# A first mixture's norm spread over other steps of a token-mixing loop, and real matmuls in the place of matmuls of zeros behind it

## The reference, cut to what matters

```python
h = h + _L0_attn_ref(_layernorm(h, axis=-1), ...)
h = h + _L0_ffn_ref(_layernorm(h, axis=-1), ...)

def _layernorm(x, axis=-1, eps=1e-05):
    m = jnp.mean(x, axis=axis, keepdims=True)
    v = jnp.var(x, axis=axis, keepdims=True)
    return (x - m) / jnp.sqrt(v + eps)

def _L0_ffn_ref(x, Wr, br, ln_g, ln_b, W1, b1, W2, b2):
    logits = xt @ Wr + br
    probs = jax.nn.softmax(logits, axis=-1)
    top_p, top_idx = jax.lax.top_k(probs, TOP_K)          # TOP_K = 2 of 8 experts
    mu = xt.mean(axis=-1, keepdims=True)
    var = ((xt - mu) ** 2).mean(axis=-1, keepdims=True)
    xn = (xt - mu) * jax.lax.rsqrt(var + LN_EPS)
    h = jax.nn.gelu(jnp.einsum('end,edh->enh', xe, W1) + b1[:, None, :], approximate=False)
    ...

def _pinv(a, iters=6):
    ...
    for _ in range(iters):
        az = a @ z
        z = 0.25 * z @ (13.0 * I - az @ (15.0 * I - az @ (7.0 * I - az)))
```

## Time and profile before

| what | value |
|---|---|
| median of three executions | 708.01 us |
| lowest and highest | 704.61, 708.11 us |
| the profiled execution's own time | 709.06 us |
| its span in the trace | 707.3 us |
| mean granted TensorE clock over the span | 0.972 of full |

### The profile page before, as it was taken

One profiled execution on the slowest core, in us unless ns is written; L12 is line 12 of the kernel. 1 busy time (PEld: TensorE's weight loads), 2 busy tenths in 40 slices (PEclk: granted clock), 3 DMA queues, 4 the chain that ended last, 5 costly groups with the idle time before them and its releaser, 6 DMA issues. The chain is left out here.

```text
span 707.3 us, 15186 instructions
## 1 busy us (share of the span) xinstructions
PE 662.3 (94%) x6053; PEld 509.3 (72%) x6053; DVE 408.3 (58%) x832; ACT 375.1 (53%) x1033; POOL 229.6 (32%) x204
## 2 busy tenths in 40 slices
PE   9988989999999999999989999789999999999895
PEld 5777888898989898989755555467666666658555
DVE  3457575758585757665742333346777777754331
ACT  4667685746565555565255555235554555546431
POOL 4074443535363534444300451032232222200001
PEclk9999999999999999999999999859999999997999
DMA  8200000000000000000000000000000000000000
GB/s 278 102 3 2 1 1 2 3 1 2 1 2 2 1 2 2 1 2 2 1 1 1 1 1 1 0 1 2 1 1 1 1 0 2 1 0 1 1 16 17
DMA packets 5214, 8.23 MB, mean 12 GB/s; under 512 B 3608, under 2 KB 4120, under 8 KB 4760
## 3 DMA queue, kind: packets, MB, share of 16 engines
q1 hardware_dynamic: 4552, 7.20, 3.1%
q10 hardware_dynamic: 592, 0.07, 0.1%
HBM read 6.71 MB, written 0.55 MB: 10 GB/s over the span
## 5 line engine op out<-in xcount | busy, mean ns | idle before, releaser
L1333 POOL TENSOR_TENSOR STD<-STD,NN 91x492 f32<-91x492 f32 (+1 forms) x96 | 104.1, 1101 | 148.3 <-DVE NN L1489 79.1
L940 PE MATMUL PS<-ST 128*91 128x123 f32 x768 | 92.4, 271 | 5.3 <-DVE ST L1495 5.3
L1489 DVE SCALAR_TENSOR_TENSOR NN<-ST,PS 91x492 f32<-91x492 f32 x96 | 62.9, 661 | 57.1 <-PE PS L940 56.8
L940 PEld LDWEIGHTS PS<-ST 128*91 128x91 f32 x768 | 83.5, 159 | 10.9 <-DVE ST L1495 6.9
L940 PE MATMUL PS<-NN 128*91 128x123 f32 (+1 forms) x768 | 88.4, 266 | 2.0 <-DVE NN L1489 2.0
L940 PEld LDWEIGHTS PS<-NN 128*91 128x91 f32 x768 | 81.0, 159 | 9.0 <-DVE NN L1489 5.4
L1980 PE MATMUL PS<-QR,KA 128*128 128x270 f32 x256 | 72.5, 414 | 0.0
L2096 DVE TENSOR_SCALAR CL<-PS,K 128x270 f32<-128x270 f32 x144 | 65.6, 495 | 9.9 <-PE PS L1980 4.5
L1495 DVE SCALAR_TENSOR_TENSOR ST<-PS,STD 91x492 f32<-91x492 f32 (+1 forms) x96 | 56.0, 599 | 26.3 <-POOL STD L1333 16.4
L1212 ACT ACTIVATE STD<-ST 91x492 f32<-91x492 f32 (+1 forms) x96 | 51.6, 569 | 36.0 <-DVE ST L1495 36.0
L2037 ACT ACTIVATE EX<-CL,NG 128x540 f32<-128x540 f32 x64 | 46.7, 741 | 32.8 <-DVE CL L2096 32.7
(11 more groups left out here) (347 smaller groups left out, 1215.7 us busy)
## 6 DMA issues: line engine op xcount, KB each, us to landing
TP<-taps SPq DMA_DIRECT2D x1, 1204.0 KB, 15.6
MA<-mat SPq DMA_DIRECT2D x1, 1120.0 KB, 7.6
MF<-mat SPq DMA_DIRECT2D x1, 1024.0 KB, 12.6
WI<-wide SPq DMA_DIRECT2D x1, 902.0 KB, 9.1
CO<-const SPq DMA_DIRECT2D x1, 512.0 KB, 16.0
MQ<-mat SPq DMA_DIRECT2D x1, 512.0 KB, 16.6
out<-OS SPq DMA_DIRECT2D x8, 45.0 KB
XA<-xpatch SPq DMA_DIRECT2D x1, 256.0 KB, 2.8
```

What stands on the lines that cost most here:

```text
L940: last = nc.tensor.matmul(PS[0:NL, PINV + q, h % 4 * SW + c0:(h % 4 + 1) * SW], x[:, h, 0:NL], x[:, h, c0:SW], start=True, stop=True)
L1333: nc.gpsimd.tensor_tensor(TD[:, 4 * q:4 * q + 4, c0:SW], SA[:, 4 * q:4 * q + 4, c0:SW], NN[0:NL, 4 * q:4 * q + 4, c0:SW], ALU.subtract).th ...
L1489: v.scalar_tensor_tensor(out=NN[0:NL, own, :], in0=ST[0:NL, b % 2, own, :], scalar=N_S, in1=heads4(PS[0:NL, PINV + q, 0:4 * SW]), op0=ALU. ...
```

## The change: pieces in other steps, and the scales' matmuls in the tail

Nothing is computed otherwise. The pieces of the norm stand behind other steps:

| piece | engine | step before | step after |
|---|---|---|---|
| `spreads` (variances) | TensorE | 5 | 6 |
| `rooted` | ScalarE | 6 | 8 |
| `router` | TensorE | 7 | 9 |
| `inverted` | VectorE | 7 | 9 |
| `widths` | ScalarE | 9 | 10 |
| `scales` | TensorE | 10 | in the tail, one pair at a time |
| `rescaled` | VectorE | 11, ahead of the second part of the rank | pair 0 behind that part, pairs 1 and 2 at the block's end |

The three calls of `spin` in the tail (12 matmuls of 512 columns) are gone. In their places stand `scale(0)`, `scale(1)` and `scale(2)`, with three matmuls of 90 columns each. The variances and roots of the fourth pair use bank `NORMS` in place of bank 1.

```diff
-                def scales():
-                    for p in EARLY:
-                        pe.wait_ge(sem("d_widened"), p + 1)
-                        spread(p, p).then_inc(sem("d_spread"), 1)
-
-                NORM = {1: centred, 5: spreads, 7: router, 10: scales}
+                def scale(p):
+                    pe.wait_ge(sem("d_widened"), p + 1)
+                    spread(p, p).then_inc(sem("d_spread"), 1)
+
+                NORM = {1: centred, 6: spreads, 9: router}
...
                 attend(B - 1, 0)
                 attend(B - 1, 1)
-                pe.wait_ge(sem("d_step"), 1)
-                spin(2, NORMS)
+                scale(0)
                 out_proj(B - 1)
-                spin(4, NORMS)
+                scale(1)
                 pe.wait_ge(sem("f_res"), upto(B - 1, 3, 3))
-                pe.wait_ge(sem("d_done"), BP - 1)
+                pe.wait_ge(sem("d_done"), 1)
                 centre(BP - 1, 0).then_inc(sem("d_centred"), 1)
                 pe.wait_ge(sem("d_squared"), BP)
-                variances(BP - 1, 1, KT * (BP - 1)).then_inc(sem("d_var"), 1)
-                spin(6, NORMS)
+                pe.wait_ge(sem("d_step"), 1)
+                variances(BP - 1, NORMS, KT * (BP - 1)).then_inc(sem("d_var"), 1)
+                scale(2)
...
-                NORM.update({2: squared, 6: lambda: rooted(EARLY, NORMS), 9: widths})
+                NORM.update({2: squared, 8: lambda: rooted(EARLY, NORMS), 10: widths})
...
-                NORM = {2: (kept_early,), 7: (inverted,), 10: (ranked_first,),
-                        11: (rescaled, lambda: ranked(dve, "d", EARLY, NORMS, 1))}
+                NORM = {2: (kept_early,), 9: (inverted,), 10: (ranked_first,),
+                        11: (lambda: ranked(dve, "d", EARLY, NORMS, 1), lambda: rescaled(0))}
...
                 residual(B - 1)
                 kept(BP - 1, 0)
+                rescaled(1)
+                rescaled(2)
```

More of the change, by code:

```diff
@@ L1312, in _ @@
                 squares(BP - 1, 0).then_inc(sem("d_squared"), 1)
-                rooted(LATE, 1)
+                rooted(LATE, NORMS)
             @block.gpsimd
@@ L1471, in ranked_first, with rescaled @@
                     ranked(dve, "d", EARLY, NORMS, 0)
[L1473 to L1476, removed]
-                NORM = {2: (kept_early,), 7: (inverted,), 10: (ranked_first,),
-                        11: (rescaled, lambda: ranked(dve, "d", EARLY, NORMS, 1))}
+                def rescaled(p):
+                    dve.wait_ge(sem("d_spread"), p + 1)
+                    normalised(p, p).then_inc(sem("d_done"), 1)
+                NORM = {2: (kept_early,), 9: (inverted,), 10: (ranked_first,),
+                        11: (lambda: ranked(dve, "d", EARLY, NORMS, 1), lambda: rescaled(0))}
                 def body(b):
```

## The result

The changed kernel took 711.51 us, the median of 20 executions (706.38 to 720.06), against 708.44 us for the kernel before in 20 executions run beside them (704.61 to 720.23). The ratio is 1.0056, with a 95% interval of 1.0031 to 1.0080: slower by 0.6%, or some 4 us (3.07 us between the medians). The forecast was 708.5 us and no change, with a range that ended at 711.5 us. Executions in the slow state (of both kernels) are left out of each ratio, though not of the medians.

What follows compares the result with a forecast made beforehand. TensorE, busy 94% of the span, was taken as the bound. 709.06 - 1.0 (loop -0.46, block's end -0.5) + 1.5 (clock) = 709.6 us; with the median 1.05 us under the profiled time, 708.5 us, range 704.9 to 711.5 us.

Steps and rivals of the forecast that it cites:

- Variances and logits moved: Loop, step 4 to step 10: variances and logits in later steps start step 10 earlier; -1.32 + 0.06 + 0.80 = -0.46 us.
- The reading of the 0.42 us ahead of step 10: TensorE's idle 0.42 us before step 10: it waits for VectorE's `ST`, reached over GpSimd slightly later than TensorE's two steps.
- Scales out of step 10: Step 10 to `attend`: frees 1.98 us of TensorE, counted as 0 because VectorE's rank ends level; bounds 0 and -1.98 us.
- the 6.2 us that were to be a sign of being wrong: Loop's end: the prediction called itself wrong if `attend` started less than 6.2 us behind step 10; it expected 6.32 us.
- Block's end 0.5 us earlier: Tail: `scale(2)` of 0.66 us replaces 1.63 us of zeros, VectorE ends about 359.5 us; -0.5 us, bounds 0 and -0.5 us.
- The clock falls once more, for one stretch of 3.4 us: Tail into the mixture: TensorE's clock falls to 0.50 for at least one such stretch; +1.5 us; chance 0.47.
- The bound of 1.7 us: Mixture's first microseconds: the most that 3.4 us at half speed can lose; the lower bound was 0.9 us.
- The first gap changes little in this trace: Ahead of `attend`: idle time grows from 1.04 to 3.0 us, but the clock falls there already; put at nothing.
- The rival that was slower (711.8 us): Tail into mixture: clock stays low from 350 to about 368 us; +1.5, +3.3 and -1.0 us make +3.8 us; chance 0.12.
- The rival's reason for doubt: Behind the loop: against one long low stretch, the clock rose at 353.7 us on the strength of `attend` alone.
- The rule named from the Trainium skill: Tail: clock drops only behind an idle gap much longer than expected at 359 us, so nothing is lost there; 707.0 us.

Runs made afterwards that it cites:

- e4: The kernel before with only the table of moved pieces changed; scales stay behind step 10 and the tail keeps its zeros; ratio to before 1.0018.
- e5: The changed kernel with 8 matmuls of zeros ahead of `attend` and none in the tail; ratio to before 1.0004.
- e3: The kernel before with e4's table, all scales and 2 matmuls of zeros behind step 11, tail zeros kept; ratio 0.9988, median 705.76 against 707.01 us.
- e1: The kernel before without the tail's 12 matmuls of zeros, nothing in their place; ratio to before 1.0050, median 710.27 against 707.01 us.
- e2: The changed kernel with 2, 3 and 6 matmuls of zeros behind `scale(0)`, `scale(1)` and `scale(2)`; ratio to before 1.0037.
- e7: The changed kernel with 6 matmuls of zeros behind `scale(2)` alone, at the block's end; ratio to before 1.0053.
- e10: The changed kernel with 8 matmuls of zeros ahead of `attend` and, behind `scale(1)` and `scale(2)`, zeros fitted to the waits; ratio to before 1.0012.
- e9: e8 with 2 more zeros ahead of and 2 behind the last centring, 3 for 5 ahead of the second attention's first projection; ratio to before 0.9923.
- e8: e3 with matmuls of zeros added where the mixture's block ends and the second attention begins; ratio to before 0.9967.

## Why the prediction was wrong

- *Variances and logits moved: -0.46 us.* Right: -0.41 us from step 4 to step 10, in e4 too. The reading of the 0.42 us ahead of step 10 left something out: on VectorE the residual of the batch before (L1447) ended at 343.37 us, later than GpSimd's half, and the `ST` that step 10 waited for began at 343.40 us. It changes nothing in the sum.
- *Scales out of step 10: worth 0, VectorE's rank is level with them.* Right. `attend` moved by 0.14 us, to 6.18 us behind step 10 (just under the 6.2 us that were to be a sign of being wrong), but e4 has the same 6.18 us with the scales in step 10: the 0.14 us come from the table. TensorE's idle time ahead of `attend` grew to 2.68 us.
- *Block's end 0.5 us earlier.* The sign was right, the size less: 0.2 us from `attend` on. The three matmuls of `scale(2)` took 0.88 us, not 0.66 us, and the last `rescaled`, which waits for them, 0.44 us, not 0.37 us.
- *The clock falls once more, for one stretch of 3.4 us: +1.5 us.* This is the step that failed. That it falls, and where, was right. Its length was taken from the shortest stretch of the trace, and it lasted 10.2 us in both traces of the changed kernel. That cost 3.55 us, and 13.00 - 9.62 = 3.38 us in the second. The bound of 1.7 us held for one stretch of 3.4 us only and was no bound for the term: the trace of before had stretches of 23.9 us and, from 640.5 us on, of 10.2 us. With 3.55 in place of 1.5 the same sum gives 708.5 + 2.05 = 710.6 us, and with -0.75 us up to the next block in place of -1.0 us 710.8 us. Why the stretch lasted 10.2 us, and 3.4 to 13.7 us in other kernels, is open.
- *The first gap changes little in this trace.* A second term, and it was put at nothing. True of the profiled execution of before, which lost the clock under `attend` too; some of its executions likely keep it (see above; argued, not shown). e5 fills only this gap and is back at 1.0004, so the gap did cost. Between the traces of the changed kernel and of e5 `attend` itself makes 1.59 us, and the shorter stretch behind it (3.4 us in place of 10.2 us) 13.17 - 10.67 = 2.50 us; how often either falls so, the traces don't say. Of the 4.0 us of the ratio, -0.75 and 3.55 us leave 1.2 us; this gap may be a part of them.
- *The rival that was slower (711.8 us) had the right size with another mechanism.* I let one low stretch run from 350 us through the tail. In both traces of the changed kernel the clock was at 1.00 again at 354 us and fell a second time near 360 us. The rival's reason for doubt (the clock rises on the strength of `attend`) held, and the loss came from a second fall.

The rule named from the Trainium skill, "TensorE: Matmul & The Clock Gate", section "Why this matters for your kernels", names only longer idle gaps than the 1.73 us at the end of the tail, so by it the clock would have stayed up there. The trace of the changed kernel disagrees: the clock fell at 360.25 us, 1.3 us into that stretch, with 0.49 us of idle time and narrow matmuls (2 and 90 columns) ahead of it.

## What to carry to other kernels

When filler is taken from TensorE, look not only at the time it took but at what the next dense stretch will run at; here zeros that cost 0.5 us (from `attend` to the next block 9.19 us in e3 with them, 8.68 us in e1 without, both at full clock) were worth 3 us, since the low stretch reached some 10 us into the dense work behind. Where TensorE waits anyway, put real work there and fill what is left up to the end of the wait (e3), and no further: scales and filler longer than the waits made the tail 1.41 us longer (e2). A slot freed on one engine is worth nothing while another engine's chain ends at the same moment; check both lists side by side before moving work out of it. And before you price a fall of the clock from one trace, look at the mean clock of the other executions: the trace may have lost it where others don't.

## What the runs showed of the hardware

- The lost time goes with the low time. At the mixture's start 3.4 us low cost 1.05 us (e5: 369.55 - 358.88 against 9.62 us), 6.9 us 2.5 us (e7), 10.2 us 3.55 us, 13.7 us, 3.1 us of it ahead of the block, 3.8 us (e1). Over the 20 executions of the changed kernel the shortest had a span of 704.6 us at a mean clock of 0.974, the longest 718.3 us at 0.950. That is some 37 and 72 us low, 13.7 us of time for 35 us.
- The same work ahead doesn't give the same clock each time: `attend` behind 1.03 us of idle time ran at 0.50 in before and at 1.00 in e1, with the same lists up to there. In the two traces of the changed kernel the clock fell at 350.0 us and at 349.0 us, with `attend` at 350.06 us and 349.70 us.
- A fall can come in dense work: in e7 at 362.7 us and in e10 at 361.8 us, 1.8 and 0.4 us into the mixture's block.
- Matmuls of zeros of 512 columns between thin pieces went with a clock that stayed up: in e9's trace it read 1.00 from 448 us to 456 us, where e8 with fewer of them had lost it at 451.9 us, in its trace though not in all of its executions.
